# A fused attention and mixture-of-experts layer: raw tokens in place of normalised ones

## The chip, the cores and the metric

One core of one Trainium2 chip runs the whole kernel. The metric is the device time of one execution in microseconds (us); the median of three runs of the kernel before is 363.37 us (362.83 to 364.01).

## The reference, cut to what matters

The input is 8 sequences of 1024 tokens of 128 numbers, in fp32. Each token is normalised, and the normalised token `xn` feeds an attention without softmax and a layer of eight experts, of which each token uses one:

```python
xn = (x - mean(x)) / sqrt(var(x) + 1e-5)
# attention: 16 heads of 8, chunks of 64
q, k, v = split(xn @ W_qkv);   k = (k - mean(k)) / sqrt(var(k) + 1e-5)   # per head
inter  = einsum('bhde,bthe->bthd', S, q_c)                    # S: sum over earlier chunks of v k^T
intra  = einsum('bhts,bshd->bthd', where(causal, q_c @ k_c, 0), v_c)
attn   = (inter + intra) @ W_o
# experts: the token's best centroid chooses one
e      = argmax(xn @ centroids.T);   a = sigmoid(xn @ centroids[e])
h      = relu((layernorm(xn) * ln_g[e] + ln_b[e]) @ w1[e].T + b1[e])
ffn    = a * (xn + h @ w2[e].T + b2[e]) + (1 - a) * xn        # = xn + a * (h @ w2[e].T + b2[e])
out    = x + attn + ffn
```

## The kernel before

The 8192 tokens are 64 tiles of 128. A chunk `c` of the work is one tile of each of the 8 sequences; a *quad* `n` (16 of them) is four tiles, half a chunk, and the main loop runs over 32 halves of a quad, `h = 2n` and `2n + 1`. All engines work in the order in which their programs are written; semaphores hold them together. TensorE (PE in the profile) projects q, k and v of quad `n + 1`, forms the scores, the products with the values and the output of quad `n`; VectorE (DVE) masks the scores (`score_mask`, L856), scales the values (`v_scale`, L843), masks the change of the state (`dstate_first`, `dstate_second`) and adds the residual (`result`, L889); ScalarE (ACT) evacuates PSUM; GpSimd (POOL) masks the scores that ScalarE copied, updates the state and sends token rows.

Two places where TensorE waits for VectorE matter below. `q_project(n + 1)` overwrites a PSUM bank that `dstate_second(n)` reads, and that stands behind `score_mask(2n)` in VectorE's order. `inter_first(n)` (L1295) waits for `dstate_first(n)`. The three heads' groups left to VectorE are masked in one instruction of 128x1536 or 128x2048.

Tokens are normalised two chunks ahead: statistics and moments on VectorE (`ln_stats`, `ln_moments`), the root on ScalarE, and `(x - mean) * rstd` over eight tiles on three engines (`ln_norm`: five tiles on POOL, two on ACT, one on DVE), from the buffer `xin` into `rows`. TensorE transposes `rows` (`x_transpose`). In the loop this is done in quads 0 to 6. The residual `x` is loaded a second time from HBM into `res`, 256 KB for each quad (`load_resid`). Routing runs in four batches of 16 tiles (`affinities`, `choose`, `count`, `ranks`, `places`): VectorE does `choose` in quads 2, 4, 6 and at the end of 7, and `count` with `second_rstd` in the odd half of quads 2, 4, 6 and 8, right behind `result`. POOL sends each tile's rows with an indirect DMA to the expert's place in HBM (`send_rows`), between its other work.

Behind the loop stands the expert stage: 71 slots of 128 token rows, each transposed, multiplied by `w1`, passed through ReLU, multiplied by `w2`, and scattered with an accumulating indirect DMA into the output (L494).

At the start TensorE runs 22 transposes of the identity that nobody reads (`keep_busy`, L1151), and 9 more a little later. The first tokens arrive, VectorE takes their statistics, and the normalised tiles are transposed and projected.

## Time and profile before

| | |
|---|---|
| median of three runs | 363.37 us |
| the profiled execution's own time | 364.02 us |
| its span in the profile | 362.3 us |
| PE, PEld (weight loads) busy | 94%, 81% |
| DVE, ACT, POOL busy | 78%, 67%, 69% |
| granted TensorE clock | 0.994 of full speed, mean over the span |
| moved by DMA | 33.18 MB, 92 GB/s mean |

The attention loop ends near 217 us and the expert stage takes the rest. A row of the timeline gives start, length, engine, line and what it writes from what, and in brackets how long the engine was idle just before and who ended the wait. "issue" is a wait for nothing that the profile shows. Lengths of neighbours overlap by some 0.1 us, so the step from one start to the next is what an instruction costs its engine.

### The profile page before, as it was taken

What the parts mean: (1) busy time and instruction counts of PE and PEld (TensorE: products, weight loads), DVE (VectorE), ACT (ScalarE), POOL (GpSimd) and SP (SyncE); (2) the same over time, 40 slices, a digit from 0 to 9 for tenths busy, and PEclk for the clock granted to TensorE, in tenths of its full rate; (3) what the DMA queues carried; (4) which work ended last, traced back from release to release, by engine and by line L of the source; (5) the groups of instructions that cost most, each with busy time, mean ns of one, the idle gap of its engine ahead of it and who ended that gap; (6) DMA issues with size and microseconds to landing.
All of it is one profiled execution on the core that took longest, in us unless ns stands there. A gap on an engine that the chain in (4) does not pass through costs nothing.

```text
span 362.3 us, 17501 instructions
## 1 busy us (share of the span) xinstructions
PE 341.5 (94%) x6868; PEld 293.6 (81%) x6868; DVE 283.4 (78%) x799; ACT 242.3 (67%) x657; POOL 250.6 (69%) x245
## 2 busy tenths in 40 slices
PE   7798999989999999999999989999999999999991
PEld 6466787767687687778868878999999999999990
DVE  8887898897785887977878786788877778777760
ACT  4787687777577667666665735766777767766660
POOL 3488477898797865455555503888888888888884
PEclk9999999999999999999999999999999999999997
DMA  7220333536314031445453435555555555555420
GB/s 196 70 62 19 105 91 112 178 104 187 105 48 120 26 99 52 149 131 159 132 158 94 133 86 144 67 74 71 69 69 71 72 73 69 71 76 60 36 24 0
DMA packets 55153, 33.18 MB, mean 92 GB/s; under 512 B 5352, under 2 KB 52768, under 8 KB 55072
## 3 DMA queue, kind: packets, MB, share of 16 engines
q1 hardware_dynamic: 42800, 23.53, 23.5%
q0 software_dynamic: 12272, 8.54, 17.1%
q8 instruction: 55, 0.90, 1.1%
q14 instruction: 26, 0.21, 0.2%
HBM read 18.72 MB, written 13.78 MB: 90 GB/s over the span
## 4 chain that ended last, share of the span: by engine, by line
issue 26%; PE 18%; POOL 12%; DVE 1%; ACT 1%; POOLq 1%; DVEq 0%; ACTq 0%
POOL out_dram L494 12%; PE sc L1274 4%; PE bank L1328 3%; PE bank L1337 2%; PE bank L1222 2%; PE bank L1200 1%; PE bank L1306 1%; PE bank L1295 1%; PE bank L1209 1%; PE bank L1215 1%; POOLq L71 1%; PE bank L1255 1%; DVE pr L856 1%; PE bank L1228 1%; PE bank L1233 1%
## 5 line engine op out<-in xcount | busy, mean ns | idle before, releaser
L494 POOL DMA_INDIRECT out_dram<-qx,rows x71 | 112.7, 1588 | 36.2 <-issue 21.9
L694 ACT ACTIVATE qx<-sc,b1T 128x128 f32<-128x128 f32 x280 | 80.0, 368 | 39.6 <-PE sc L1421 39.4
L420 POOL DMA_INDIRECT slots_d<-rows,pos_i x64 | 63.1, 986 | 40.6 <-PE bank L1328 10.3
L856 DVE TENSOR_TENSOR pr<-sc,causal 128x1536 f32<-128x1536 f32 (+2 forms) x33 | 63.5, 1926 | 16.1 <-PE sc L1274 16.0
L1429 PE MATMUL bank<-tokens,qx 128*128 128x128 f32 x568 | 75.2, 275 | 0.7 <-ACT qx L694 0.7
L1421 PE MATMUL sc<-wide,tokens 128*128 128x128 f32 x560 | 74.0, 275 | 0.5 <-issue 0.5
L1429 PEld LDWEIGHTS bank<-tokens,qx 128*128 128x128 f32 x568 | 69.0, 192 | 1.1 <-ACT qx L694 1.1
L1421 PEld LDWEIGHTS sc<-wide,tokens 128*128 128x128 f32 x560 | 68.2, 192 | 0.6 <-issue 0.6
L1015 DVE COPY tokens<-xT 128x1024 f32 x71 | 52.8, 745 | 0.0
L1030 DVE SCALAR_TENSOR_TENSOR qx<-bank,rows,qx 128x128 f32<-128x128 f32 x71 | 24.8, 349 | 27.2 <-PE bank L1429 26.2
L1274 PEld LDWEIGHTS sc<-qx,kT 32*64 32x64 f32 x2048 | 32.9, 130 | 15.5 <-issue 15.0
L1274 PE MATMUL sc<-qx,kT 32*64 32x128 f32 x2048 | 40.9, 279 | 1.1 <-DVE pr L856 1.1
L1328 PE MATMUL bank<-pr,vz 128*32 128x64 f32 x2048 | 38.0, 221 | 4.0 <-issue 3.9
L537 ACT ACTIVATE qx<-bank,gmask 128x512 f32<-128x512 f32 x64 | 40.0, 679 | 0.9 <-PE bank L1200 0.8
L1328 PEld LDWEIGHTS bank<-pr,vz 128*32 128x32 f32 x2048 | 31.4, 110 | 9.1 <-issue 7.3
L412 POOL TENSOR_TENSOR pr<-pr,causal 128x512 f32<-128x512 f32 x18 | 22.9, 1275 | 8.0 <-ACT pr L568 7.5
L390 POOL TENSOR_SCALAR rows<-tokens,mv,rstd 128x128 f32<-128x128 f32 x35 | 27.6, 799 | 0.2
L1022 DVE SCALAR_TENSOR_TENSOR qx<-b2b,rows 128x128 f32<-128x128 f32 x71 | 24.6, 346 | 2.0 <-ACT rows L705 1.9
L602 ACT ACTIVATE y<-bank 128x512 f32<-128x512 f32 x16 | 9.6, 598 | 24.8 <-PE bank L1328 24.8
L1009 DVE TENSOR_SCALAR wide<-rows 128x128 f32<-128x128 f32 x71 | 19.8, 278 | 4.0 <-issue 3.0
L682 ACT ACTIVATE wide<-sc 128x128 f32<-128x128 f32 x69 | 20.3, 294 | 0.0
L1222 PEld LDWEIGHTS bank<-wqkv,xT 128*128 128x128 f32 x128 | 15.5, 191 | 4.4 <-issue 3.5
(167 smaller groups left out, 530.7 us busy)
## 6 DMA issues: line engine op xcount, KB each, us to landing
rows<-slots_d SPq DMA_DIRECT2D x71, 66.0 KB, 2.1
res<-in_L_attn_x_dram SPq DMA_DIRECT2D x16, 256.0 KB
out_dram<-res SPq DMA_DIRECT2D x16, 256.0 KB, 3.6
tokens<-in_L_attn_x_dram SPq DMA_DIRECT2D x7, 512.0 KB, 4.2
w1raw<-in_L_ffn_w_dram SPq DMA_DIRECT2D x8, 256.0 KB
w2raw<-in_L_ffn_w_dram SPq DMA_DIRECT2D x8, 256.0 KB
out_dram<-qx,rows POOLq DMA_INDIRECT x71, 3.4
slots_d<-rows,pos_i POOLq DMA_INDIRECT x64
```

Of the source, the lines that this page charges most:

```text
L390: last = pool.tensor_scalar(rows[:, t, 0:D], xin[:, c % 2, b, :], mv[:, t, 0:1], rstd[:, t:t + 1], ALU.subtract, ALU.mult)
L420: pool.indirect_dma_start(slots_d, bass.IndirectOffsetOnAxis(ap=pos_i[:, t:t + 1], axis=0), rows[:, t, :], None)\
L494: pool.indirect_dma_start(out_rows, bass.IndirectOffsetOnAxis(ap=xs[:, a, D + 2:D + 3].bitcast(U32), axis=0), ye[:, a, :], None, bounds_ch ...
L537: ins = nc.scalar.activation(qx[:, n % 2, :, j, :], FA[:, :].rearrange("p (i t) -> p i t", t=P), ACT.Copy, scale=gmask[:, j * DK:j * DK + 1])
L694: last = nc.scalar.activation(ht[:, k % 2, c * P:(c + 1) * P], inner(k)[:, c * P:(c + 1) * P], ACT.Relu, bias=b1T[:, bass.ds(e * FC + c, 1)])
L856: nc.vector.tensor_tensor(pr[:, h % 2, a:G, w].rearrange("p g (j t) -> p g j t", t=CH), sc[:, a * BANK:G * BANK].rearrange("p (g w) -> p g ...
L1015: nc.vector.tensor_copy(ws[:, k % 3, :], wts[:, bass.ds(e * WE, WE)]).then_inc(s("ws_ready"), 1)
L1030: nc.vector.scalar_tensor_tensor(out=ye[:, a, :], in0=banks[k % 2][:, 0:D], scalar=xs[:, a, D + 1:D + 2], in1=yb[:, k % 2, :], op0=ALU.mul ...
L1274: last = mm(SC[g][CH * up:CH * (up + 1), at:at + PAIRS * CH], kT[r, n % 2, tok], qx[r, n % 2, i, 2 * up:2 * up + 2, CH * c:CH * (c + 1)], ...
L1328: last = mm(Y[half][SW * g:SW * (g + 1), i * P + CH * c:i * P + CH * (c + 1)], vz[:, half, c, i, g, p, :], pr[:, h % 2, g, k:k + CH], star ...
L1421: last = mm(inner(k)[:, c * P:(c + 1) * P], ws[:, k % 3, c * P:(c + 1) * P], xsT[:, k % 2, :], start=True, stop=True)
L1429: last = mm(banks[k % 2][:, 0:D], ht[:, k % 2, c * P:(c + 1) * P], ws[:, k % 3, F + c * D:F + (c + 1) * D], start=(c == 0), stop=(c == FC ...
```

## The change

The tokens are no longer normalised. `rows` holds them as they come from HBM; TensorE transposes, projects and routes them raw, and POOL sends them raw.

- **Weights.** Centring the token is moved to the weights: the column means of `W_qkv` come from three matmuls with a matrix of 1/128 (`weight_means`), VectorE subtracts them (`wqkv_centre`), and the centroids lose their mean on VectorE. `wqkv` is loaded ahead of the tokens.
- **Deviation.** `1 / std` of the token goes into three places: the square sum of `k` gets `8 * eps * (var + eps)` added (`kadd`, in `k_var`), the scale of the values is multiplied by it (`k_rstd`), and `result` multiplies the attention's output by it, now four instructions over one tile each.
- **Residual.** The second load of `x` is gone. ScalarE writes `x * (1 + rstd) - mean * rstd` into `res` (`residual`, four instructions for each quad), which holds the residual and the `xn` that the expert stage added before.
- **Experts.** The slot's row carries a scale and a shift, so that `se_scale` restores the normalised row; `se_shift` no longer adds the row.
- **Order.** POOL's `ln_norm` is gone, and its `send_rows` keep the waits that paced them, of quads 7 and 8 in another place. Nothing waits for `xin`'s two halves any more, since tokens go straight to `rows`. At the start VectorE takes the statistics behind the weights, and those of chunk 1 (the third step) stand partly behind `v_scale(0)`.

```diff
-                sp.dma_start(xin[:, c % 2, :, :], x_v[:, c, :, :]).then_inc(s(f"x_in{c + 1}"), 16)
+                sp.dma_start(raw_rows(c, 0, B), x_v[:, c, :, :]).then_inc(s(f"x_in{c + 1}"), 16)
...
+            sp.dma_start(wqkv[:, :], w_qkv).then_inc(s("wqkv_in"), 16)
             for st, (c, lo, hi) in enumerate(STEPS[:2]):
...
-                    load_resid(n + 1)
...
+                if h % 2 and n + 1 >= NCH:
+                    pool.wait_ge(s("sc_ps"), h + 1)
+                    send_rows(1)
                 mask_scores(h)
...
-                        ln_norm(n + 2, range(4))
-                        ln_norm(n + 2, (4,))
...
+            def residual(n):
+                half = n % 2
+                act.wait_ge(s("nmr_ready"), 1 + n if n < 2 else n // 2 + 2)
+                reach(act, s(f"attn_out{half}"), 16 * (n // 2))
+                for i in range(HALF):
+                    t = first_tile(n) + i
+                    last = nc.scalar.activation(res[:, half, i, :], rows[:, t, 0:D], ACT.Identity, bias=nmr[:, t:t + 1],
+                                                scale=onep[:, t:t + 1])
+                last.then_inc(s("resid_ready"), 1)
...
+                nc.vector.tensor_scalar(kadd[:, c * B + lo:c * B + hi], mv[:, c * B + lo:c * B + hi, 1], EPS, EPS * DK,
+                                        ALU.add, ALU.mult)
+                nc.vector.tensor_scalar(onep[:, c * B + lo:c * B + hi], rstd[:, c * B + lo:c * B + hi], 1.0, None,
+                                        ALU.add).then_inc(s("nmr_ready"), 1)
+
+            def wqkv_centre(a, name):
+                dve.wait_ge(s("wmean_ps"), a + 1)
+                cols = slice(a * D, (a + 1) * D)
+                nc.vector.tensor_tensor(wqkv[:, cols], wqkv[:, cols], mean_bank(a), ALU.subtract).then_inc(s(name), 1)
...
             def k_rstd(n):
                 dve.wait_ge(s("kstd_ready"), n + 1)
-                nc.vector.reciprocal(krs[:, :], kstd[:, :]).then_inc(s("krs_ready"), 1)
+                t = first_tile(n)
+                kr = krs[:, :].rearrange("p (i h) -> p i h", h=H)
+                link(nc.vector.reciprocal(krs[:, :], kstd[:, :]))
+                nc.vector.tensor_tensor(kr, kr, bcast(rstd[:, t:t + HALF], 2, H), ALU.mult).then_inc(s("krs_ready"), 1)
...
-                dve.wait_ge(s(f"resid_in{half}"), 16 * (n // 2 + 1))
-                nc.vector.tensor_tensor(res[:, half, :, :], Y[n % 2][:, :].rearrange("p (i d) -> p i d", d=D),
-                                        res[:, half, :, :], ALU.add).then_inc(s("res_ready"), 1)
+                dve.wait_ge(s("resid_ready"), n + 1)
+                for i in range(HALF):
+                    t = first_tile(n) + i
+                    last = nc.vector.scalar_tensor_tensor(out=res[:, half, i, :], in0=Y[n % 2][:, i * D:(i + 1) * D],
+                                                          scalar=rstd[:, t:t + 1], in1=res[:, half, i, :], op0=ALU.mult,
+                                                          op1=ALU.add)
+                last.then_inc(s("res_ready"), 1)
...
-                nc.vector.reciprocal(rows[:, tiles, D], tmp_nt2[:, tiles]).then_inc(s("rows_done"), 1)
+                link(nc.vector.reciprocal(tmp_nt[:, tiles], tmp_nt2[:, tiles]))
+                link(nc.vector.tensor_tensor(rows[:, tiles, D], rstd[:, tiles], tmp_nt[:, tiles], ALU.mult))
+                nc.vector.scalar_tensor_tensor(out=rows[:, tiles, D + 3], in0=mv[:, tiles, 0], scalar=-1.0,
+                                               in1=rows[:, tiles, D], op0=ALU.mult, op1=ALU.mult).then_inc(s("rows_done"), 1)
...
-            keep_busy(22)
+            def weight_means():
+                pe.wait_ge(s("avg_ready"), 1)
+                pe.wait_ge(s("wqkv_in"), 16)
+                for a in range(3):
+                    cols = slice(a * D, (a + 1) * D)
+                    mm(mean_bank(a), avg[:, :], wqkv[:, cols], start=True, stop=True).then_inc(s("wmean_ps"), 1)
+
+            keep_busy(18)
...
+            weight_means()
             x_transpose(0, SC[0])
-            keep_busy(9)
-            pe.wait_ge(s("wqkv_in"), 16)
+            keep_busy(4)
+            pe.wait_ge(s("wq_ready"), 1)
```

**VectorE at the start.** The rows begin with `gmask`, the mask that ScalarE needs for the first q. Of the kernel before:

```order
L796 TENSOR_REDUCE gmask<-headmask 128x32 [waits pool_m]
L774 RECIPROCAL rstd<-std 128x4 [waits std_ready]
L780 SCALAR_TENSOR_TENSOR nmr<-mv,rstd 128x4 [waits rstd_ready]
L788 TENSOR_SCALAR rows<-tokens,mv,rstd 128x128 x2
L760 BN_STATS stats<-tokens 128x6 [waits x_in1]
```

And of the change, where `sc` and `bank` hold the weights' means:

```order
L775 TENSOR_REDUCE gmask<-headmask 128x32 [waits pool_m]
L777 TENSOR_REDUCE smask<-headmask 128x64
L772 TENSOR_TENSOR wqkv<-wqkv,sc 128x128 [waits wmean_ps] x2
L783 TENSOR_REDUCE tmp_nt<-wqkv 128x16 [waits wk_ready]
L784 TENSOR_SCALAR tmp_nt<-tmp_nt 128x16 [waits dve_chain]
L785 TENSOR_TENSOR wqkv<-wqkv,tmp_nt 128x128 [waits dve_chain]
L772 TENSOR_TENSOR wqkv<-wqkv,bank 128x128 [waits wmean_ps]
L741 BN_STATS stats<-rows 128x6 [waits x_in0]
```

The first statistics stood ahead of `gmask`; now they stand behind the weights, and these behind TensorE's means.

**VectorE between the first scaled values (`vp`) and the first masked scores (`pr`).** Of the kernel before:

```order
L843 TENSOR_TENSOR vp<-bank,krs 128x512 [waits krs_ready,v_ps]
L1042 TENSOR_SCALAR notbefore<-ones_v 128x128
L1043 CAST iotk<-iot_i 128x71
L1044 COPY rows<-id_i 128x64
L856 TENSOR_TENSOR pr<-sc,causal 128x1536 [waits sc_ps]
```

And of the change, where `cmean` is the centroids' mean:

```order
L826 TENSOR_TENSOR vp<-bank,krs 128x512 [waits krs_ready,v_ps]
L1035 TENSOR_SCALAR notbefore<-ones_v 128x128
L1036 CAST iotk<-iot_i 128x71
L1037 COPY rows<-id_i 128x64
L741 BN_STATS stats<-rows 128x6 [waits x_in2]
L741 BN_STATS stats<-rows 128x6 x3
L749 BN_AGGR mv<-stats 128x2 [waits stats_done]
L749 BN_AGGR mv<-stats 128x2 x7
L1043 TENSOR_REDUCE cmean<-small 8x1 [waits small_in]
L1044 TENSOR_SCALAR cmean<-cmean 8x1 [waits dve_chain]
L1045 TENSOR_SCALAR small<-small,cmean 8x128 [waits dve_chain]
L839 TENSOR_TENSOR pr<-sc,causal 128x1536 [waits sc_ps]
```

Half of the statistics of the third step, its eight moments and the centroids now stand between the two.

**VectorE in the loop, from `result(0)` to the scaled values of quad 2.** Of the kernel before:

```order
L889 TENSOR_TENSOR res<-bank,res 128x512 [waits resid_in0,out_ps]
L828 TENSOR_REDUCE kvar<-sq 128x64 [waits sq_ready]
L856 TENSOR_TENSOR pr<-sc,causal 128x1536 [waits av_ps,sc_ps]
L833 RECIPROCAL krs<-kstd 128x64 [waits kstd_ready]
L843 TENSOR_TENSOR vp<-bank,krs 128x512 [waits vz_own,ds_ps,vz_across,krs_ready,v_ps]
```

And of the change:

```order
L874 SCALAR_TENSOR_TENSOR res<-bank,rstd,res 128x128 [waits resid_ready,out_ps]
L874 SCALAR_TENSOR_TENSOR res<-bank,rstd,res 128x128 x3
L807 TENSOR_REDUCE kvar<-sq 128x64 [waits nmr_ready,sq_ready]
L809 TENSOR_TENSOR kvar<-kvar,kadd 128x64 [waits dve_chain]
L839 TENSOR_TENSOR pr<-sc,causal 128x1536 [waits av_ps,sc_ps]
L815 RECIPROCAL krs<-kstd 128x64 [waits kstd_ready]
L816 TENSOR_TENSOR krs<-krs,rstd 128x64 [waits dve_chain]
L826 TENSOR_TENSOR vp<-bank,krs 128x512 [waits vz_own,ds_ps,vz_across,krs_ready,v_ps]
```

`result` is four instructions in place of one, and two short ones that wait for their forerunner's end are added for each quad.

## Rows read from the trace of the kernel before

**Rows 1.** Busy time by stretch: PE, PEld, DVE, ACT, POOL; clock, DMA share, GB/s

```profile
15.25:18.75 3.50, 1.35 (x37) 1.01 (x36) 3.41 (x8) 2.44 (x6) 2.45 (x4) 1.00 0.00 0
30.00:50.00 20.00, 19.88 (x544) 14.87 (x533) 15.79 (x43) 16.37 (x34) 13.81 (x18) 1.00 0.21 59
224.00:350.00 126.00, 126.00 (x1132) 126.00 (x1132) 98.34 (x266) 87.91 (x340) 105.29 (x67) 1.00 0.52 68
```

**Rows 2.** Timeline of PE, start to the second q projection

```profile
1.97 4.75 PE L1151 MATMUL sc<-ident 128*128 128x128 f32 x22 [1.97 <-POOL ident L352]
7.52 1.15 PE L1151 MATMUL sc<-ident 128*128 128x128 f32 x9
...
14.15 1.10 PE L1209 MATMUL bank<-xT,wqkv 128*128 128x512 f32 x2
16.13 0.69 PE L1255 MATMUL bank<-vp,kn 64*64 64x64 f32 x32 [0.88 <-DVE vp L843]
17.58 0.65 PE L1215 MATMUL bank<-ident,kT 128*128 128x128 f32 x4 [0.76 <-ACT kT L592]
18.75 1.12 PE L1200 MATMUL bank<-xT,wqkv 128*128 128x512 f32 x2 [0.52 <-DVE dstate L870]
```

**Rows 3.** Timeline of DVE in the same stretch

```profile
4.10 0.81 DVE L760 BATCH_NORM_STATS2 stats<-tokens 128x6 f32<-128x128 f32 x4
4.95 0.38 DVE L768 BATCH_NORM_AGGREGATE mv<-stats 128x2 f32<-128x6 f32 x4
5.69 0.18 DVE L774 RECIPROCAL rstd<-std 128x4 f32<-128x4 f32 x1
...
7.69 0.25 DVE L807 TENSOR_REDUCE tmp_nt<-wqkv 128x16 f32<-128x128 f32 x1
...
8.40 0.17 DVE L774 RECIPROCAL rstd<-std 128x4 f32<-128x4 f32 x1
...
10.73 0.69 DVE L819 COPY kT<-bank 128x512 f32<-128x512 f32 x1 [1.25 <-PE bank L1209]
11.34 0.86 DVE L760 BATCH_NORM_STATS2 stats<-tokens 128x6 f32<-128x128 f32 x4
12.17 0.69 DVE L824 COPY kn<-bank 128x512 f32<-128x512 f32 x1
...
13.56 0.69 DVE L828 TENSOR_REDUCE kvar<-sq 128x64 f32<-128x512 f32 x1
14.16 0.63 DVE L768 BATCH_NORM_AGGREGATE mv<-stats 128x2 f32<-128x6 f32 x8
14.71 0.52 DVE L833 RECIPROCAL krs<-kstd 128x64 f32<-128x64 f32 x1
15.34 0.69 DVE L843 TENSOR_TENSOR vp<-bank,krs 128x512 f32<-128x512 f32 x1
...
16.29 1.75 DVE L856 TENSOR_TENSOR pr<-sc,causal 128x1536 f32<-128x1536 f32 x1
```

**Rows 4.** Timeline of PE in quad 3, `inter_first`

```profile
55.49 0.68 PE L1295 MATMUL bank<-qT,state 64*64 64x64 f32 x16 [0.41 <-DVE dstate L865]
```

**Rows 5.** Groups by line and shape: busy us, mean ns of one, idle before

```profile
L494 POOL DMA_INDIRECT out_dram<-qx,rows x71 | 112.7, 1588 | 36.2 <-issue 21.9 <-DVE qx L1030 14.2
L390 POOL TENSOR_SCALAR rows<-tokens,mv,rstd 128x128 f32<-128x128 f32 x35 | 27.6, 799 | 0.2
L1030 DVE SCALAR_TENSOR_TENSOR qx<-bank,rows,qx 128x128 f32<-128x128 f32 x71 | 24.8, 349 | 27.2 <-PE bank L1429 26.2
L889 DVE TENSOR_TENSOR res<-bank,res 128x512 f32<-128x512 f32 x16 | 11.0, 690 | 6.2 <-PE bank L1337 5.9
L518 ACT ACTIVATE rows<-tokens,nmr,rstd 128x128 f32<-128x128 f32 x18 | 7.8, 480 | 0.6 <-DVE nmr L780 0.6
```

**Rows 6.** Waits: engine, line, what it waited for; total us, times, longest

```profile
PEld sc L1274 <- issue: 15.0, 30, 1.2
...
PE bank L1328 <- issue: 3.9, 5, 1.4
```

More of the change, by code:

```diff
@@ L383, in _ @@
             sent = [0]
-            def ln_norm(st, tiles):
-                c = STEPS[st][0]
-                pool.wait_ge(s("rstd_ready"), st + 1)
-                for b in tiles:
-                    t = c * B + b
-                    last = pool.tensor_scalar(rows[:, t, 0:D], xin[:, c % 2, b, :], mv[:, t, 0:1], rstd[:, t:t + 1],
-                                              ALU.subtract, ALU.mult)
-                last.then_inc(s("lnx_pool"), 1)
             def values_own(n):
@@ L511, in ln_root @@
                     .then_inc(s("std_ready"), 1)
-            def ln_norm(st, tiles):
-                c = STEPS[st][0]
-                act.wait_ge(s("nmr_ready"), st + 1)
-                for b in tiles:
-                    t = c * B + b
-                    last = nc.scalar.activation(rows[:, t, 0:D], xin[:, c % 2, b, :], ACT.Identity, bias=nmr[:, t:t + 1],
-                                                scale=rstd[:, t:t + 1])
-                last.then_inc(s("lnx_act"), 1)
+            def residual(n):
[7 more added lines that the diff above has]
+                last.then_inc(s("resid_ready"), 1)
             def xT_copy(u, bank):
@@ L652, in _ @@
                         k_square(n + 1)
-                    if norm:
-                        ln_norm(n + 2, (5, 6))
                     if n in (2, 4, 6, 8):
@@ L675, in _ @@
                         values_own(n + 1)
+                    residual(n)
                     if n == 0:
@@ L759, in ln_stats @@
                 for b in tiles:
[L760 removed]
+                    last = nc.vector.bn_stats(stats[:, c % 2, b, :], rows[:, c * B + b, 0:D])
                 if tiles[-1] == hi - 1:
@@ L797, in _ @@
                                     op=ALU.add).then_inc(s("masks_ready"), 1)
-            ln_inverse(0)
-            ln_shift(0)
-            ln_norm(0, (2, 3))
-            ln_stats(1, range(*STEPS[1][1:]))
-            ln_moments(1)
-            dve.wait_ge(s("wqkv_in"), 16)
+            nc.vector.tensor_reduce(out=smask[:, :], in_=headmask[:, :].rearrange("p (g k) -> p k g", k=GW), axis=AX,
+                                    op=ALU.add)
+            wqkv_centre(0, "wq_ready")
+            wqkv_centre(1, "wk_ready")
+            dve.wait_ge(s("wk_ready"), 1)
             wk = wqkv[:, D:2 * D].rearrange("p (h d) -> p h d", d=DK)
@@ L808, in _ @@
             link(nc.vector.tensor_scalar(tmp_nt[:, 0:H], tmp_nt[:, 0:H], 1.0 / DK, None, ALU.mult))
-            nc.vector.tensor_tensor(wk, wk, bcast(tmp_nt[:, 0:H], 2, DK), ALU.subtract).then_inc(s("wqkv_ready"), 1)
-            ln_inverse(1)
-            ln_shift(1)
-            ln_norm(1, (6, 7))
-            nc.vector.tensor_reduce(out=smask[:, :], in_=headmask[:, :].rearrange("p (g k) -> p k g", k=GW), axis=AX,
-                                    op=ALU.add)
+            nc.vector.tensor_tensor(wk, wk, bcast(tmp_nt[:, 0:H], 2, DK), ALU.subtract).then_inc(s("wk_ready"), 1)
+            wqkv_centre(2, "wv_ready")
+            ln_stats(0, range(*STEPS[0][1:]))
+            ln_moments(0)
+            ln_inverse(0)
+            ln_shift(0)
             def kT_copy(n):
@@ L1034, in _ @@
             kT_copy(0)
+            ln_stats(1, range(*STEPS[1][1:]))
+            kn_copy(0)
+            ln_moments(1)
+            k_var(0)
+            ln_inverse(1)
+            ln_shift(1)
             ln_stats(2, range(4))
-            kn_copy(0)
-            ln_stats(2, range(4, B))
-            k_var(0)
-            ln_moments(2)
             k_rstd(0)
@@ L1044, in _ @@
             nc.vector.tensor_copy(rows[:, :, D + 2].bitcast(I32), id_i[:, :])
+            ln_stats(2, range(4, B))
+            ln_moments(2)
+            cen = small[E * FC:E * FC + E, :]
+            mean = cmean[E * FC:E * FC + E, :]
+            dve.wait_ge(s("small_in"), 64)
+            link(nc.vector.tensor_reduce(out=mean, in_=cen, axis=AX, op=ALU.add))
+            link(nc.vector.tensor_scalar(mean, mean, 1.0 / D, None, ALU.mult))
+            nc.vector.tensor_scalar(cen, cen, mean, None, ALU.subtract).then_inc(s("cen_ready"), 1)
             for h in range(NH):
@@ L1067, in _ @@
                         ln_shift(n + 2)
-                        ln_norm(n + 2, (7,))
                     if stat:
```

84 lines of the change are left out of this document (33 added, 51 removed).

## The prediction

> **What bounds the kernel now.** Read the busy time by stretch first. In the attention loop TensorE works 19.88 of 20 us while VectorE works 15.79, ScalarE 16.37 and GpSimd 13.81; in the expert stage TensorE and its weight loads fill 126 of 126 us [rows 1]. So from some 20 us on a saving counts only where it ends a wait of TensorE, and any added wait of TensorE is added to the end. Then read TensorE's timeline at the start, the one stretch where it has room: from 15.25 to 18.75 us it works 1.35 of 3.50 us while VectorE works 3.41 [rows 1], and its waits end with `vp`, with `kT` and with `dstate` [rows 2]. The second q projection at 18.75 stands behind VectorE's first masked scores, which start at 16.29 because VectorE had something to do nearly all the time before [rows 3]. The start is bound by VectorE's order, the rest by TensorE.
>
> In the expert stage GpSimd is close behind: a scatter takes 1.588 us and 21.9 us of idle over 70 of them add 0.31, so 1.90 us for each slot [rows 5]. The change leaves both the matmuls and the scatter as they are. The stage keeps its length and only begins earlier or later.
>
> **The start.** The change lets TensorE transpose raw tokens early, but VectorE now begins with the weights, and these need TensorE's means, which stand behind 18 transposes of the identity. 22 of them took 4.75 us from 1.97 on [rows 2], so 18 end at 1.97 + 18 x 0.216 = 5.86. A mean's matmul isn't in the trace; between one and two such transposes and a semaphore, 0.3 to 0.6 us, gives the first centred weights at 6.2 to 6.5, and I take 6.5. Before, VectorE's layer norm began at 4.10 [rows 3].
>
> From there I walk VectorE's new order with the steps of the old one [rows 3], each from start to start. Two centrings and the heads' mean of the k weights, which took 7.69 to 8.40 before: until 7.95; the third centring 0.25: 8.2. Four statistics, 0.85 (4.10 to 4.95): 9.05. From the moments to the reciprocal 0.74 (4.95 to 5.69): 9.8. The reciprocal with now three short instructions behind it, estimated from its 0.18 and 0.08 for each that waits for nothing: 10.25. `kT` 0.61 (10.73 to 11.34): 10.9, as early as before, since VectorE idled 1.25 us there. Four statistics 0.83: 11.75. `kn` 0.6: 12.35. Four moments 0.3, then the square on ScalarE, which kept `kvar` until 13.56 before and now until about 13.15. `kvar` 0.6 and the added sum 0.2: 13.95. Reciprocal and shifts of the second step 0.5: 14.45. Four statistics 0.83: 15.3. `krs` 0.63 (14.71 to 15.34) and the product with the tokens' deviation 0.2: 16.1. `vp` and the three short ones 0.95 (15.34 to 16.29): 17.05. Then what has been put in between: four statistics 0.83, eight moments 0.55 (14.16 to 14.71), the centroids' three instructions with two waits 0.65 (as for the heads' mean): 19.1. The masked scores start at 19.1 in place of 16.29, and with them the second q projection at about 21.55 in place of 18.75. **Start: +2.8 us**, between +1.5 (means at 6.2, each estimated step shorter) and +4.0 (every wait on a forerunner 0.1 us longer). The removed tiles of `ln_norm` are already out of this sum. Between about 19 and 21.55 TensorE has nothing it may do. On SP's queue the weights move ahead of the tokens; these had landed by 4.10 [rows 3], and their statistics now begin at 8.2, so that costs nothing.
>
> **The loop.** On VectorE, `result` becomes four instructions of 128 columns from PSUM. The nearest row takes 0.349 us against 0.690 for the one of 512 [rows 5]; with 0.1 us of overlap each, 1.05 against 0.6: +0.45 for each quad. The sum behind `kvar` and the product behind `krs` are +0.2 each, `second_rstd` has two more that wait, +0.4 for each batch, and one tile of `ln_norm` leaves, at most -0.3. In all some +0.6 to +1.0 us for a quad of 12.4 us (16 of them between 18.75 and some 217), and 4.2 of 20 us were free, so VectorE does not become the bound as a whole.
>
> It matters where VectorE is late already. In quad 3 TensorE waited 0.41 us for `dstate` [rows 4], and ahead of that stand `result`, `count` and `second_rstd` without a wait. What is added there, 0.45 + 0.4 and about 0.15 of the short ones before it, goes straight to the path: +1.0. Quads 5, 7 and 9 have the same order, but no wait on VectorE in the row; I take half there, +0.5 each, between 0 and +1.0. **Loop: +2.5 us**, from +1.0 to +4.0.
>
> **What leaves.** POOL loses 35 instructions of 0.799 us, 27.6 us [rows 5]. I price that at nothing: no wait of TensorE in these rows ends with POOL. ScalarE loses 18 tiles of 0.480 us and takes 64 of them for the residual [rows 5]: +22 us over 16 quads, 1.4 for each. It stands behind the copies that TensorE waits for, ahead of the next quad's `kT`, whose transposes come later in TensorE's order; I take nothing, and +0.3 for each quad, +5 in all, if that cover is gone. In quads 7 and 8 a send moves ahead of a mask on POOL; at the scatter's price, 1.59 and 0.31 [rows 5], the mask is 1.9 us later, and the products that need it come half a quad, 6 us, later: nothing. The second load of the tokens, 16 of 256 KB, leaves a DMA that was used to 0.21 in the loop [rows 1]; nothing waits for it by a semaphore.
>
> One thing could give something back. In the middle of its products TensorE stood still five times, 3.9 us in total, waiting for nothing that the profile shows [rows 6]. If traffic delays what it waits for there, fewer loads help. I take a quarter: **-1.0 us**, between 0 and -3.9.
>
> **Sum.** 2.8 + 2.5 - 1.0 = +4.3. The profiled execution took 364.02 us, 362.3 of them in the span, so it would take 368.3; it lies 0.65 above the median of 363.37, and for the median that gives **367.7 us**.
>
> **A rule on the clock.** The first 22 transposes took 0.216 us each and the nine at 7.52 took 0.128 [rows 2], as at the lower and the higher of TensorE's two levels, though the column of the granted clock reads full speed from the start. From 15.25 to 18.75 TensorE was busy for 39%, and it did not slow down: two projections took 1.10 us before and 1.12 after. In the changed kernel the same 1.35 us of work would lie in 6.3 us, 21%. The Trainium skill, page "TensorE: Matmul & The Clock Gate", section "What's actually happening", says that the array falls back to half its rate when it has been idle. No row here shows a fall in mid-kernel; by that rule the time would be the first rival's.
>
> **Rivals.**
> 1. *Slower still: TensorE loses its rate in the long wait at the start.* For it: 21% against 39%. Against it: two bursts of work lie in the stretch. Price by the rows: as many instructions as at the start, 22 x (0.216 - 0.128) = +1.9, so 369.6 us.
> 2. *No change.* The start costs its 2.8, the loop's additions find cover in all quads but 3 (+1.0), and the halts all go, -3.9: 363.3 us. For it: VectorE's free 4.2 of 20 us. Against it: the free time lies behind TensorE, not ahead of the batches' masks.
> 3. *Faster: the second load of the tokens is what made TensorE stand still.* Its weight loads waited another 15.0 us in 30 pieces ahead of the scores, again for nothing shown [rows 6]. If the 3.9 go and a third of the 15.0 with them, -8.9 + 5.3 = -3.6, so 359.8 us. It decides from 5.3 us recovered of these 18.9. Against it: TensorE is busy 19.88 of 20 us, so the weight loads wait under running matmuls.
> 4. *The change does not do what it says*: the loop's POOL or ScalarE work stays on a path that I don't see, and VectorE's start is hidden after all because the first q projection gates instead. Then the numbers are those of the second rival, and its chance holds both.
>
> **Chances.** Forecast 0.55, first rival 0.19, second and fourth 0.13, third 0.13. A change of 0.3%, 1.1 us, is about what a measurement of this kernel can tell. Forecast and first rival are slower by more than that: 0.74. The second is the same, 0.13; the third faster, 0.13. The forecast's own range, from its terms' nearer bounds, is 365.5 to 370.0. The wider one leaves out the third rival almost whole and the far end of the first, and reaches from 363.2 to 371.0.
>
> **What would show it.** On VectorE's timeline the first masked scores near 19 us and TensorE's second q projection near 21.5; if they stand below 18 and 20.5, my walk is wrong. In quad 3 `inter_first` waits for `dstate` some 1.4 us; without that wait, the loop's term is wrong. TensorE's halts with "issue" in the products below 3.9 us. A granted clock below full speed, or projections of 2 us for a pair, between 21 and 28 us would show the first rival. The expert stage should keep 1.90 us for each slot; if that moves, the forecast fails at a place where I put nothing.

## The result, and the profile after

The changed kernel takes 374.47 us in the median of four runs (373.31 to 374.77), the kernel before 363.62 (362.83 to 364.01). The ratio is 1.0295, with a 95% interval from 1.0267 to 1.0324: 10.85 us slower, where 4.3 were forecast, and above the range's upper end of 371.0. The profiled execution took 374.34 us, 372.4 of them in the span (before: 364.02 and 362.3).

The span is split at three starts that any trace shows: the second q projection, the scores of the second quad (a third group of 64 matmuls) and the last scores.

| stretch | before, us | after, us | difference |
|---|---|---|---|
| begin to the second q projection | 18.75 | 21.61 | +2.86 |
| from there to the second quad's scores | 6.34 | 8.35 | +2.01 |
| loop: to the last scores | 185.74 | 190.98 | +5.24 |
| last scores to the span's end | 151.47 | 151.46 | 0 |

**The start.** VectorE's timeline of the changed kernel, which answers to [rows 3]:

```profile
15.82 0.69 DVE L826 TENSOR_TENSOR vp<-bank,krs 128x512 f32<-128x512 f32 x1
...
18.83 0.28 DVE L1045 TENSOR_SCALAR small<-small,cmean 8x128 f32<-8x128 f32 x1
19.14 1.76 DVE L839 TENSOR_TENSOR pr<-sc,causal 128x1536 f32<-128x1536 f32 x1
```

The masked scores start at 19.14; the walk gave 19.1. TensorE's timeline, which answers to [rows 2] and, further down, to [rows 4]:

```profile
13.45 1.10 PE L1213 MATMUL bank<-xT,wqkv 128*128 128x512 f32 x2
16.61 1.13 PE L1259 MATMUL bank<-vp,kn 64*64 64x64 f32 x32 [2.06 <-DVE vp L826]
18.06 1.12 PE L1219 MATMUL bank<-ident,kT 128*128 128x128 f32 x4 [0.32 <-ACT kT L576]
21.61 2.08 PE L1204 MATMUL bank<-xT,wqkv 128*128 128x512 f32 x2 [2.44 <-DVE dstate L853]
23.62 2.01 PE L1278 MATMUL sc<-qx,kT 32*64 32x128 f32 x64
25.55 1.56 PE L1332 MATMUL bank<-pr,vz 128*32 128x64 f32 x64
...
61.62 0.68 PE L1299 MATMUL bank<-qT,state 64*64 64x64 f32 x16 [1.53 <-DVE dstate L848]
...
89.78 0.68 PE L1299 MATMUL bank<-qT,state 64*64 64x64 f32 x16 [1.48 <-DVE dstate L848]
...
151.27 0.65 PE L1237 MATMUL bank<-ident,w2raw 128*128 128x128 f32 x4 [0.61 <-DVE vp L826]
```

Two waits for VectorE, 2.06 and 2.44 us, stand in this stretch. From the first on every instruction takes nearly twice as long: the 32 of the state step 1.13 us (0.69 before), the q projection 2.08 (1.12). The windows, which answer to [rows 1] (the columns are the same), say why:

```profile
16.00:17.00 1.00, 0.39 (x15) 0.42 (x19) 1.00 (x6) 0.45 (x2) 0.35 (x1) 0.66 0.00 0
17.00:26.00 9.00, 6.24 (x117) 3.82 (x116) 7.24 (x29) 4.04 (x8) 2.92 (x5) 0.50 0.00 0
26.00:28.00 2.00, 2.00 (x64) 1.91 (x56) 1.97 (x3) 2.00 (x5) 1.28 (x1) 0.86 0.03 8
30.00:50.00 20.00, 19.33 (x573) 13.79 (x578) 16.41 (x58) 16.20 (x36) 7.14 (x9) 1.00 0.17 44
224.00:350.00 126.00, 125.24 (x1168) 124.09 (x1167) 99.57 (x269) 85.99 (x331) 97.65 (x62) 1.00 0.53 74
```

The granted clock was 0.50, the lower level of 1.2 GHz, from 17 to 26 us. All four runs of the changed kernel show a mean clock of 0.977 to 0.985 over their span; of 23 runs of the kernel before in a later session, 17 show 0.991 or more and six 0.982 to 0.989, so a fall is rarer there, but not absent (g4_no_reload below shows one). This is the first rival, on top of the forecast. In the expert stage nothing moved. The waits and groups that answer to [rows 5, 6] (waits: total us, times, longest; groups: busy us, mean ns of one):

```profile
PEld sc L1278 <- issue: 16.6, 32, 1.5
...
PE bank L1299 <- DVE dstate L848: 4.0, 4, 1.5
...
PE bank L1332 <- issue: 1.1, 3, 0.5
```

```profile
L477 POOL DMA_INDIRECT out_dram<-qx,rows x71 | 112.9, 1590 | 36.0 <-issue 22.0 <-DVE qx L1021 14.0
...
L502 ACT ACTIVATE res<-rows,nmr,onep 128x128 f32<-128x128 f32 x64 | 26.3, 485 | 0.2
...
L874 DVE SCALAR_TENSOR_TENSOR res<-bank,rstd,res 128x128 f32<-128x128 f32 x64 | 18.0, 344 | 3.5 <-PE bank L1341 3.2
```

A slot still takes 1.590 and 0.31 us. TensorE's halts without a shown cause ("issue") fell in the products from 3.9 us to 1.1; some stand in other instructions now, and in the whole loop they fell from 3.9 to 2.3. In their place stand waits for `dstate`: 4.0 us in four, in quads 3, 5, 8 and 9, where the loop before had 0.85 in two, that of [rows 4] and one in quad 8. The first line is of the kernel before, the second of the changed one:

```profile
122.44 0.68 PE L1295 MATMUL bank<-qT,state 64*64 64x64 f32 x16 [0.44 <-DVE dstate L865]
```

```profile
142.37 0.68 PE L1299 MATMUL bank<-qT,state 64*64 64x64 f32 x16 [0.56 <-DVE dstate L848]
```

### The profile page after: what moved, and what is told of

It is laid out like the page before. It is cut to its first block, busy times and chain, and to the rows that moved or that the text cites. A ratio compares the mean times of both kernels' runs of the same rounds, so it can differ in the third digit from the quotient of the medians.

```text
span 372.4 us, 17609 instructions
## 1 busy us (share of the span) xinstructions
PE 344.6 (93%) x6865; PEld 294.2 (79%) x6865; DVE 301.6 (81%) x904; ACT 257.7 (69%) x703; POOL 222.9 (60%) x210
## 4 chain that ended last, share of the span: by engine, by line
issue 30%; PE 28%; DVE 21%; POOL 13%; ACT 3%; DMA 2%; SPq 1%; POOLq 1%; DVEq 0%; ACTq 0%
POOL out_dram L477 12%; PE sc L1278 5%; DVE pr L839 5%; PE bank L1332 4%; PE bank L1204 3%; PE bank L1226 2%; PE bank L1341 2%; PE bank L1213 2%; PE bank L1299 2%; PE bank L1310 1%; PE bank L1219 1%; DVE stats L741 1%; DVE res L874 1%; PE bank L1259 1%; DVE kvar L807 1%
## 5 line engine op out<-in xcount | busy, mean ns | idle before, releaser
L1006 DVE COPY tokens<-xT 128x1024 f32 x71 | 54.7, 771 | 0.2 <-issue 0.2
L1000 DVE TENSOR_SCALAR wide<-rows 128x128 f32<-128x128 f32 x71 | 24.0, 339 | 3.3 <-issue 2.7
L502 ACT ACTIVATE res<-rows,nmr,onep 128x128 f32<-128x128 f32 x64 | 26.3, 485 | 0.2
L566 ACT ACTIVATE vz<-vp 64x256 f32<-64x256 f32 x16 | 6.7, 417 | 22.1 <-DVE vp L826 22.1
L1013 DVE TENSOR_SCALAR qx<-b2b,rows 128x128 f32 x71 | 20.3, 286 | 1.2 <-ACT rows L686 1.0
L874 DVE SCALAR_TENSOR_TENSOR res<-bank,rstd,res 128x128 f32<-128x128 f32 x64 | 18.0, 344 | 3.5 <-PE bank L1341 3.2
```

The costliest lines, as they stand in the source:

```text
L502: last = nc.scalar.activation(res[:, half, i, :], rows[:, t, 0:D], ACT.Identity, bias=nmr[:, t:t + 1], scale=onep[:, t:t + 1])
L1006: nc.vector.tensor_copy(ws[:, k % 3, :], wts[:, bass.ds(e * WE, WE)]).then_inc(s("ws_ready"), 1)
```

## The experiments

The table has all of them: the median, the interval of the ratio to the kernel before on the same chip, and from the profiled run the start of the second quad's scores and the length of the loop as defined above. A loop length carries one to two us of such halts by chance, so the medians decide. The edits are shown shortened, some in words.

| kernel | median, us | ratio to before, 95% | quad 2 at | loop |
|---|---|---|---|---|
| before / after | 363.62 / 374.47 | 1.0267-1.0324 | 25.09 / 29.96 | 185.74 / 190.98 |
| e1_fill | 371.11 | 1.0173-1.0232 | 27.62 | 189.17 |
| e2_order | 372.43 | 1.0206-1.0266 | 27.05 | 191.84 |
| e3_result_one | 373.25 | 1.0236-1.0298 | 29.77 | 190.60 |
| e4_residual_one | 373.71 | 1.0234-1.0296 | 30.79 | 189.82 |
| f1_start | 373.04 | 1.0222-1.0294 | 27.24 | 192.33 |
| f2_vector | 370.49 | 1.0154-1.0228 | 27.23 | 188.09 |
| f3_scalar | 372.43 | 1.0179-1.0271 | 28.49 | 192.05 |
| f4_both | 369.84 | 1.0109-1.0216 | 26.91 | 188.40 |
| g1_before_vector | 373.39 | 1.0209-1.0296 | 27.46 | 193.17 |
| g2_before_shift | 363.81 | 0.9974-1.0039 | 26.51 | 184.30 |
| g3_start_all | 375.71 | 1.0263-1.0364 | 28.99 | 188.63 |
| g4_no_reload | 363.93 | 0.9971-1.0027 | 26.43 | 185.12 |
| j1_before_k | 370.96 | 1.0172-1.0230 | 27.25 | 190.10 |
| j2_before_result | 363.77 | 0.9983-1.0030 | 25.15 | 185.49 |
| j3_before_short | 366.05 | 1.0046-1.0100 | 25.29 | 188.77 |
| j4_before_scalar | 364.12 | 0.9990-1.0037 | 26.51 | 185.75 |
| r1_roots | 373.12 | 1.0192-1.0245 | 30.80 | 189.99 |
| r2_roots_pool | 371.25 | 1.0154-1.0206 | 30.87 | 187.54 |

### The clock and the start

**e1_fill.** Transposes of the identity in the two waits:

```
+ if n == 0: wait_ge(xT_sb, 2); fill(Y[0], 14)      # ahead of state_step(0)
+ if n == 0: fill(Y[1], 16)      # ahead of q_project(1)
```

> The changed kernel with 14 transposes of the identity in TensorE's wait ahead of the first state step (14.5 to 16.6 us) and 16 in the one ahead of the second q projection (19.2 to 21.6 us); nothing else. Theory clock: TensorE's fall to the lower level is what the second half of the lost start is made of. Then the second q projection takes 1.1 us in place of 2.08 and still starts near 21.6, the scores behind it 1.2 in place of 2.01, the scores of the second quad start at 27.8 in place of 29.96, and the time is 372.3 us (-2.1). Rival late VectorE: the long instructions hide behind the masks anyway, the scores of the second quad still start near 29.9, and the time stays within 0.5 of 374.5.

TensorE's timeline:

```profile
13.81 1.69 PE L1155 MATMUL bank<-ident 128*128 128x128 f32 x14
16.04 0.69 PE L1263 MATMUL bank<-vp,kn 64*64 64x64 f32 x32 [0.54 <-issue]
17.49 0.65 PE L1223 MATMUL bank<-ident,kT 128*128 128x128 f32 x4 [0.76 <-ACT kT L576]
17.98 1.91 PE L1155 MATMUL bank<-ident 128*128 128x128 f32 x16
21.03 1.12 PE L1208 MATMUL bank<-xT,wqkv 128*128 128x512 f32 x2 [1.14 <-DVE dstate L853]
```

The clock stays at 1.00 and the projection takes 1.12 us. From it to the second quad's scores are 6.59 us in place of 8.35: 1.8 us are the clock's, as the theory had it (the projection began 0.6 earlier). The median fell by 3.4. By this one profile, which is 4.1 us shorter, the rest is not the clock: 0.6 us come ahead of the edit (the first transposes took 3.60 us in place of 4.10), and 1.8 from a loop with fewer halts (0.2 us in place of 2.3).

**e2_order.** VectorE's moved work goes behind the masks:

```
-  ln_stats(2, range(4, B)); ln_moments(2); (centroids' mean)   # behind notbefore, iotk
   score_mask(0); dstate_first(0); dstate_second(0)
+  ln_stats(2, range(4, B)); ln_moments(2); (centroids' mean)
```

> The changed kernel with VectorE's second half of statistics, moments of the third step and centring of the centroids behind the first masked scores and the two dstate instructions instead of ahead of them. Theory walk: these stood for 2.4 us on the path; masked scores at 16.8 in place of 19.14, second q projection at 19.3 in place of 21.61, time 372.1 us (-2.4) if the clock has already fallen in the first wait (14.5 to 16.6) and comes back no earlier, and 370.0 (-4.5) if the shorter second wait keeps or brings back the higher level. Rival: the moved work only delays the next step (kn on ScalarE behind the third root), and the scores of the second quad start at most 1 us earlier: 373.5 or more.

The second q projection started at 18.64, 3.0 us earlier; 0.5 of that lie in the first transposes (3.58 us in place of 4.10), and about 2.4 are left for the moved work, as the theory priced it. The second quad's scores stood 2.9 us earlier, and the median was 2.0 lower. The walk's term is real. The clock still fell (0.64 from 18 to 20 us, 0.51 from 20 to 22).

**f1_start** and **g3_start_all** put the two together; g3 adds 4 transposes in the second wait and moves a root on ScalarE behind the square of `k`.

> The changed kernel with both mends of the start: 14 transposes of the identity in TensorE's wait ahead of the first state step, and VectorE's moved statistics, moments and centring behind the first masked scores and dstate. Theory: walk and clock add up; the second q projection starts near 18.6 us and takes 1.1, the scores of the second quad start near 25.5 (25.09 before, 29.96 in the changed kernel), and what is left above the kernel before is the loop's: 374.5 - 2.9 - 1.6 = 370.0 us. Rival: the earlier start only meets a longer wait in the loop, 371.5 or more.

> f1_start with 4 more transposes ahead of the second q projection, and the root of the third step on ScalarE behind the square of k instead of ahead of kn. Theory: in f1_start the clock fell in the second wait and qT came late because the moved moments held back kn on ScalarE; with both mended the second q projection takes 1.1 us at 18.7, the scores of the second quad start near 24.5 in place of 27.24, and the time is 370.3 us. Rival: the clock still falls (projections of 2 us): 372 us or more.

Both missed. f1_start's loop was 1.4 us longer than the changed kernel's, as the rival had it, and its clock fell in spite of the fill, as its windows show:

```profile
18.00:20.00 2.00, 1.49 (x5) 0.53 (x3) 1.97 (x13) 0.00 (x0) 1.63 (x3) 0.73 0.00 0
20.00:22.00 2.00, 2.00 (x49) 1.22 (x54) 1.83 (x14) 1.71 (x4) 0.00 (x0) 0.50 0.00 0
```

In g3_start_all it held until 26 us and fell then, behind a wait of 1.80 us for `qT`. Its six runs spread from 370.3 to 377.0 us, and the profiled one is the fastest of them, so whether and why it is the slowest is not settled. f2_vector, f3_scalar and f4_both below have f1_start's fill and order at the start; in the trace of the first the clock held at 1.00, in the other two it fell from 26 us on.

So the waits alone do not say when the clock falls. The plainest case is g4_no_reload (below), which leaves the start of the kernel before as it was:

```profile
1.97 4.05 PE L1151 MATMUL sc<-ident 128*128 128x128 f32 x22 [1.97 <-POOL ident L351]
...
18.75 2.08 PE L1200 MATMUL bank<-xT,wqkv 128*128 128x512 f32 x2 [0.52 <-DVE dstate L869]
```

From 14 us on TensorE's instructions start at the times of [rows 2], to the hundredth, with the same waits of 0.88, 0.76 and 0.52 us. Yet in that trace the clock held, and here it was 0.65 from 18 to 20 us and 0.50 from 20 to 22, and the second quad's scores stood at 26.43 in place of 25.09. What differs ahead is that the first 22 transposes took 4.05 us in place of 4.75. Why the clock fell in one and not in the other is open.

### Which engine's work the loop pays for

**e3_result_one, e4_residual_one** make one 128x512 instruction of `result` and of ScalarE's residual.

```
-  four scalar_tensor_tensor (res <- Y, rstd, res)      # e3
+  tensor_tensor(res[:, half], Y[n % 2], res[:, half], ADD)
-  four activation(res[:, half, i], rows[:, t], ...)    # e4
+  activation(res[:, half], rows[:, t:t + HALF], ...)
```

> The changed kernel with `result` as one 128x512 addition; the factor of the tokens' deviation on the attention's output is left out. VectorE saves about 0.4 us for each of 16 quads. Theory VectorE: the four instructions delay the masked scores and dstate of quads 3, 5, 7 and 9, and TensorE's waits of 1.5 us for dstate there shrink by 0.4 each: 372.9 us (-1.6). Rival ScalarE: the loop's loss comes through ScalarE's copies (its residual): within 0.5 of 374.5.

> The changed kernel with the residual as one 128x512 ScalarE instruction for a quad; the factors of the first of its four tiles are used for all four. ScalarE saves some 0.5 us for each of 16 quads. Theory ScalarE: the residual stands ahead of the next quad's first copies, and TensorE's waits for xT in the second half of the loop (0.25 us and more for each quad) go with it: 372.0 us (-2.5). Rival VectorE: within 0.5 of 374.5.

Both gave back about 1 us, with intervals that overlap the change's, so neither is told from nothing. In e3_result_one the waits for `dstate` in the loop fell from 4.0 to 3.05 us, of which 0.4 in quad 3, as its theory had it; in quad 5 nothing fell.

**f2_vector, f3_scalar, f4_both** take more out, on f1_start:

```
-  tensor_tensor(kvar, kvar, kadd, ADD); tensor_tensor(krs, krs, rstd, MULT)   # f2, f4, and result as in e3
-  residual(n)                                                                # f3, f4
```

> f1_start with VectorE's additions to the loop taken out: `result` as one 128x512 addition, no sum behind `kvar`, no product behind `krs` (the factors of the deviation are left out). VectorE saves about 1 us a quad, ScalarE nothing. Theory VectorE: the loop's loss (some 5 us) is VectorE's lateness in the masked scores and dstate of the quads with routing and in vp of quads 9 to 12; 3.5 us go: 366.5 us. Rival ScalarE: less than 1 us goes: 369 or more.

> f1_start with ScalarE's residual taken out: `result` adds the raw tokens in place of it (the normalized tokens are left out of the sum). ScalarE saves 1.6 us a quad, VectorE nothing. Theory VectorE: less than 1 us goes: 369 or more. Rival ScalarE: the residual delays the copies of k and so kvar and vp; 3 us go: 367.0 us.

> f1_start with both taken out: VectorE's additions and ScalarE's residual (`result` one addition of the raw tokens). If the additions of the two engines are all of the loop's loss, the loop is as long as before's and the time is 365.0 us or less (before, with the start's remaining 0.5). If it is more than 1 us above that, something else in the change costs (GpSimd's order, the tokens' raw rows, the place of the code fetches).

VectorE's additions give back 2.55 us in the median, with intervals that just touch; the loop falls from 192.33 to 188.09, in f2_vector's fastest run. The windows of the loop, f1_start's and then f2_vector's:

```profile
27.24:219.57 192.33, 179.97 (x5118) 137.14 (x5118) 166.12 (x489) 145.79 (x308) 99.90 (x111) 1.00 0.29 84
```

```profile
27.23:215.32 188.09, 179.42 (x5118) 137.97 (x5118) 153.99 (x419) 145.66 (x308) 99.77 (x111) 1.00 0.29 86
```

VectorE was 12.1 us less busy, and by these profiles a third of that came off the path, by the medians a fifth. The waits for `vp` went (1.8 us in f1_start's loop, none here); those for `dstate` hardly did (3.9 and 3.4). ScalarE's 22 us (f3_scalar) give back 0.6, within the uncertainty. f4_both is still 5.6 us above the kernel before: in the profile the start's 1.8, and in the loop 2.7 that neither edit had touched. About 0.8 of these are the clock's, which fell there from 26 us on: from the second quad's scores to the third's it took 8.15 us, and 7.31 in f2_vector.

**g1, j1, j2, j3, j4** go the other way: parts of the change, made neutral by factors of one, on the kernel before.

```
j1 +  tensor_tensor(kvar, kvar, zero, ADD); tensor_tensor(krs, krs, one, MULT)
j2 +  result as four scalar_tensor_tensor with a factor of one
j3 +  two in ln_shift, one in choose, two in second_rstd
g1 =  j1 + j2 + j3        j4 +  four activations on res for each quad
```

> The kernel before with the change's additions on VectorE alone, made neutral by factors of one and a sum of zero: `result` as four instructions from PSUM, a sum behind `kvar`, a product behind `krs`, two more in ln_shift, one in choose, two in second_rstd. TensorE's code, the start's order, ScalarE, GpSimd and the loads stay. Theory VectorE: this is the loop's loss; +4 us: 367.8 us, with some 0.6 of it at the start. Rival: the loop's loss comes from the rest of the change; within 1.5 us of 363.8.

> The kernel before with the sum behind `kvar` (of zero) and the product behind `krs` (by one) alone. Theory chain: these two stand in the chain kvar, krs, vp and ahead of the second scores' copies, which TensorE waits for; they are the larger part of g1's 9.7 us: +5 or more, 368.7 us. Rival VectorE's time: each part costs in proportion to its time (0.45 us a quad of about 1.1): +4.0, 367.7 us. Rival threshold: VectorE has room for one part but not for all; under +1.5 us.

> The kernel before with `result` as four instructions (by a factor of one) alone. Theory chain: result stands behind vp and its cost only shows in the quads with routing; +2, 365.7 us. Rival VectorE's time (0.42 us a quad): +3.8, 367.5 us. Rival threshold: under +1.5 us.

> The kernel before with the short additions alone: two in ln_shift, one in choose, two in second_rstd (neutral factors). Theory chain: they stand ahead of the masked scores of the quads with routing, 0.44 us in four of them, and 0.15 in eight: +1.5, 365.2 us. Rival VectorE's time: +1.9, 365.6. Rival threshold: under +1.0 us.

> The kernel before with ScalarE's residual alone (four instructions a quad, in place, by a factor of one, behind the second load of the tokens), at its place in the changed kernel. ScalarE gets 25 us more. Theory VectorE: ScalarE's residual is hidden: within 1 us of 363.7. Rival ScalarE: it holds back the copies of k and so VectorE's chain: +3 us or more.

VectorE's additions alone cost 9.7 us. Of these j1 has 7.4 (6.3 to 8.4), j3 2.5 (1.7 to 3.6), j2 and j4 nothing that can be measured. No theory of cost by busy time holds on this kernel: j2 adds 6.8 us of VectorE's time in the loop for nothing, j1 10.6 us for 7.4. What differs is the place: the parts of j1 stand between the square of `k` and `vp`, and TensorE waits for `vp` before it may overwrite the bank that holds v. j1's three engines, VectorE first, then GpSimd, then TensorE:

```profile
77.39 1.37 DVE L842 TENSOR_TENSOR krs<-krs,one 128x64 f32<-128x64 f32 x1
78.85 0.69 DVE L852 TENSOR_TENSOR vp<-bank,krs 128x512 f32<-128x512 f32 x1
...
92.10 1.62 DVE L842 TENSOR_TENSOR krs<-krs,one 128x64 f32<-128x64 f32 x1
...
106.18 1.40 DVE L842 TENSOR_TENSOR krs<-krs,one 128x64 f32<-128x64 f32 x1
```

```profile
73.37 4.08 POOL L393 TENSOR_SCALAR rows<-tokens,mv,rstd 128x128 f32<-128x128 f32 x5
77.42 1.25 POOL L415 TENSOR_TENSOR pr<-pr,causal 128x512 f32<-128x512 f32 x1
...
92.38 1.26 POOL L415 TENSOR_TENSOR pr<-pr,causal 128x512 f32<-128x512 f32 x1
...
106.24 1.26 POOL L415 TENSOR_TENSOR pr<-pr,causal 128x512 f32<-128x512 f32 x1
```

```profile
79.59 0.66 PE L1175 MATMUL bank<-ident,rows 128*128 128x128 f32 x4 [1.28 <-DVE vp L852]
...
94.56 0.65 PE L1175 MATMUL bank<-ident,rows 128*128 128x128 f32 x4 [0.57 <-DVE vp L852]
...
108.42 0.66 PE L1175 MATMUL bank<-ident,rows 128*128 128x128 f32 x4 [1.10 <-DVE vp L852]
```

A product of 0.22 us takes 1.37, 1.62 and 1.40 where GpSimd's mask runs beside it, and ends 0.1 us behind that; TensorE's wait for `vp` follows each time. The Trainium skill, page "SBUF — State Buffer", section "SBUF: two separate sides", says that a VectorE instruction with two SBUF inputs and a GpSimd instruction that reads SBUF exclude each other for their whole length; the rows agree, with 1.37 to 1.62 us in place of 0.22.

The three waits are 2.95 us. They are not all of j1's 7.4: in its profile the second quad's scores stand 2.2 us later, with the clock at 0.50 to 0.86 from 18 to 24 us, and the loop is 4.4 longer. That the collisions make up the larger part of the loop's loss is read from the timelines; no run moves GpSimd's mask out of the way.

In the changed kernel the same collision is there once in full, not three times: without its five tiles of `ln_norm` ahead of the mask, GpSimd is through by then. The one, VectorE and then GpSimd:

```profile
134.78 1.17 DVE L816 TENSOR_TENSOR krs<-krs,rstd 128x64 f32<-128x64 f32 x1
```

```profile
134.58 1.28 POOL L398 TENSOR_TENSOR pr<-pr,causal 128x512 f32<-128x512 f32 x1
```

So j1's 7.4 us are not the change's, where the sum behind `kvar`, the product behind `krs` and `result` together gave back 2.55. What all these parts share is the wait for `dstate` in the loop: 0.85 us before, 1.9 in j1 and in j2, 2.8 in j3 and 4.5 in g1. In j2's profile halts shrink by as much (2.7 us in place of 3.9), so that it costs nothing.

**r1_roots, r2_roots_pool** try a repair, on e1_fill: the deviation goes into ScalarE's root, as four roots with each tile's scale and shift, which VectorE prepares with one more short instruction; r2 also moves three short products to GpSimd.

```
-  activation(kstd, kvar, Sqrt, scale=1/DK)
+  four activation(kstd[i], kvar[i], Sqrt, bias=kbias[t], scale=ksc[t])
-  VectorE: rows[D+1] *= rstd; rows[D] = rstd * tmp; rows[D+3] = ...    # r2: on GpSimd
```

> e1_fill with the deviation of the keys folded into ScalarE's root: four roots of 16 columns with each tile's scale and shift in place of one of 64, so that the sum behind `kvar` and the product behind `krs` leave VectorE; ln_shift gets one more short instruction. The result is the reference's. Theory chain: these two are the larger part of the loss in the changed kernel too (7.4 us alone on the kernel before): 371.1 - 5 = 366.1 us, between 364.5 and 367.5. Rival: in the changed kernel other things take their place (f2_vector gave back 2.5 us for them and result together): 368.5 us or more.

> r1_roots with the short additions of choose and second_rstd moved to GpSimd (three products of 16 columns at the start of each batch's scatters). The result is the reference's. Theory: they cost 2.6 us alone on the kernel before, some 1.5 of it from these two: 364.6 us, about the kernel before. Rival: GpSimd's products delay the scatters or masks: no gain over r1_roots.

r1 missed: it is no faster than e1_fill (1.0218 against 1.0203 of the kernel before). The waits of TensorE show one new place:

```profile
PE bank L1174 <- ACT qT L530: 3.3, 7, 1.0
PE bank L1236 <- ACT qT L530: 1.1, 2, 0.7
```

The four roots stand ahead of `qT` on ScalarE, and 4.4 us of waits for it came, 3.65 of them in the loop, where those for `vp` went (1.75 in e1_fill). The larger loss stands at the start: the second quad's scores start at 30.80 in place of 27.62, while the loop is only 0.8 us longer. There the new scale's first instruction, of 128x4, took 1.88 us beside two GpSimd memsets of 1.84 (14.28 to 16.16 us), the added one waits for its end, and `vp` came at 17.77 in place of 15.24. r2 has the same late start. So the repair does not tell what the pair costs in the changed kernel. r2 is 1.9 us faster than r1 in the median and 1.4 by the ratios, whose intervals overlap; its loop is 2.45 shorter. The short products on VectorE seem to cost about that in the changed kernel too.

### The halts without a shown cause

**g2_before_shift** moves TensorE's code by 6 matmuls, **g4_no_reload** takes 14 of the 16 second loads away.

```
g2 +  6 transposes of the identity ahead of state_step(0)
g4 -  load_resid(n + 1)
```

> The kernel before with 6 transposes of the identity in TensorE's wait of 0.9 us ahead of the first state step, which move all of TensorE's later code by 6 matmuls. Theory code place: the halts without a shown cause come at fixed places of TensorE's code; the five of 0.91, 1.44, 0.83, 0.18 and 0.58 us move to other instructions, and in quad 5 the wait for dstate shows instead of the halt of 1.44. Time between 362 and 364.5 us. Rival traffic: they stay at their times (near 29, 80, 95, 139 and 185 us) and sizes.

> The kernel before without the second load of the tokens beyond the first two quads (the sum uses what lies in the buffer; the residual is left out): 14 of 16 loads of 256 KB gone. Theory traffic: the halts without a shown cause (3.9 us) shrink by half or more: 362 us or less. Rival code place: they stay at the same instructions with the same sizes within 0.4 us: 363.3 to 364.3 us.

TensorE's timeline in quad 5, of g4 and then of g2:

```profile
82.53 0.99 PE L1328 MATMUL bank<-pr,vz 128*32 128x64 f32 x56 [1.47 <-issue]
```

```profile
82.65 0.68 PE L1295 MATMUL bank<-qT,state 64*64 64x64 f32 x16 [1.18 <-DVE dstate L865]
```

Without the loads the longest halt stands at the same instruction, behind 8 of 64 products, with 1.47 us (before 1.44). All halts of the loop came to 2.8 us in place of 3.9, within what traces with the loads show (2.0 to 4.2 in j2, j3 and j4), and the time did not fall: the second load of the tokens does not make them. With the code moved the longest is gone, and the wait for `dstate` that it had covered shows. That halts belong to places in TensorE's code is likely, since that one stands behind the same 8 of 64 products in j2, j3 and j4 (0.5 to 0.9 us). It is not shown: j1_before_k, with the code where it was, has no halt there either. That they are late fetches of code (the profile has a queue of instructions with 55 packets and 0.90 MB) is not shown either. Both medians are the kernel before's. In g2's profile the loop is 1.4 us shorter, and the start as much longer, since the clock fell there too (0.71 from 18 to 20 us, 0.50 to 22).

## Why the prediction was wrong

**The start, +2.8: right.** Masked scores at 19.14 for 19.1, the q projection at 21.61 for 21.55; e2_order confirms the cause. That it fits to 0.04 us is luck: `vp` came at 15.82 for 16.1, and what was put between it and the scores took 3.3 us for 3.0.

**The clock, in the forecast at nothing: wrong.** It stood as a rival with 0.19, against it "two bursts of work lie in the stretch". They did not help: in the trace the clock was at 0.58 from 16 to 18 us, behind the wait of 2.06 us for `vp`, and stayed at 0.50 to 26; the mean clock of the other three runs fits that. The rival's size was right, 1.9 priced, 2.0 by the split and 1.8 by e1_fill, but by luck: the price was the count of the start's transposes, not of the work that fell to the lower level.

**The loop, +2.5: mis-sized.** Measured are 5.2 with the halts in it, where +2.5 and -1.0 were forecast. TensorE's idle time in the loop grew by 4.6 us: waits for `dstate` by 3.1, for `vp` by 0.9, for ScalarE's copies (`xT`, `smallT`) by 1.1, halts by -1.6, and the rest in gaps too short for the list of waits. The `dstate` term itself was nearly right: quad 3 +1.1 (1.53 us late, 1.4 forecast), quad 5 +1.5, quad 9 +0.6, quad 7 nothing, for +2.5 in all. Without the halts the loop's term is +6.9. Two things failed. "No wait on VectorE in the row", for quad 5: the wait was hidden in the halt of 1.44 us [rows 6], which g2 uncovers; it came to 1.48 and not to the half that was put. And "+0.2 each" for the sum behind `kvar` and the product behind `krs` went into VectorE's busy time, with "VectorE does not become the bound as a whole", and no wait for `vp` was asked about; `result` with its 0.45 was put on the path. On the kernel before j1 and j2 show it the other way round: `result` costs nothing, the short pair is what counts. In the changed kernel the two were not told apart: by f1 and f2 the pair and `result` are worth 2.5 us together (4.2 in the profiles), by e3 `result` alone 1.2, within the uncertainty, and by r1 and r2 the short products 1.4 to 2.45.

**What leaves.** ScalarE at nothing: right (j4, f3). GpSimd's 27.6 us at nothing: "no wait of TensorE in these rows ends with POOL" (but for the first, ahead of the transposes [rows 2]) looked at one step only. VectorE's new product would have waited for GpSimd's mask, as in j1; by the timelines the removed tiles prevented that. How much it is worth in the whole change was not measured. **The halts, -1.0: a size met by luck.** They fell by 1.6 us in the loop, but not because the loads are gone: g4 took 14 of them away and the time stayed, and with it rival 3's mechanism fell. In quad 5 the halt only made room for the wait that it had covered.

**The sum.** 2.9 + 2.0 + 5.2 = 10.1 us, the difference of the spans. The forecast's own range of 365.5 to 370.0 does not follow from the bounds that its terms name (1.5 + 1.0 - 1.0 and 4.0 + 4.0 - 1.0 give 364.9 and 370.4), but the result lies above either. What stays open is what makes the clock fall and when (f1 against f2, g4 against the kernel before), and the 2.7 us of f4's loop, for which the clock's 0.8 and the short products would be enough, though no run joins them. None of the versions of the changed kernel beats the kernel before.

## What to carry to other kernels

Price an added instruction by its place in the chain that the bottleneck waits for, and by what runs beside it there, not by its engine's free time: on the kernel before 0.4 us a quad behind `kvar` and `krs` cost 7.4 us, and 0.45 us of `result` nothing. A halt or a wait in the profile covers what is late behind it, so ask of each what comes next when it goes. Where work is moved ahead of what TensorE waits for, price the wait twice, as time and as a loss of its clock. Filling the waits can hold the clock (e1_fill) but is no guarantee (r1_roots has the same fills, and there it was 0.61 and 0.54 from 20 to 24 us).

## What was not expected of the hardware

- A VectorE product of 0.22 us took up to 1.62 beside a GpSimd instruction of 1.26 (j1).
- The clock was at 0.50 for 9 us behind a wait of 2.06 us. In g4_no_reload it fell behind waits of 0.88, 0.76 and 0.52 us, and with the same waits at the same times it held in the kernel before.
- TensorE's longest halt kept its instruction and its size (1.47 us for 1.44) with 14 loads of 256 KB taken away.
